# Gated delta-rule kernel: the broadcast of the pair rows in two parts by rows, two transfers under way at most, and beta multiplied in part by part

## The chip, the cores and the metric

The kernel runs on one core of a Trainium2 chip. The metric is the device time of one execution in microseconds (us). The engines are TensorE (PE; its weight loads are PEld), VectorE (DVE), ScalarE (ACT), GpSimd (POOL) and SyncE (SP). SP issues most DMAs. Each engine runs its own list of instructions in order and waits on semaphores.

## What is computed

A layer of 16 heads (head size 32) over 4 sequences of 2048 tokens of width 512: layer norm, a gated delta-rule recurrence, output projection, layer norm, residual; then a feed-forward part in which each token takes one of 16 columns. The part that the change touches is the recurrence, cut here from the reference:

```
q, k, v, gate = projections of the normed x;  beta = sigmoid(x @ Wb.T);  alpha = exp(-exp(A_log) * softplus(...))
def step(S, inp):
    k_t, q_t, v_t, beta_t, a_t = inp
    S = S * a_t[..., None, None]
    kv_mem = einsum('bhd,bhde->bhe', k_t, S)
    delta = (v_t - kv_mem) * beta_t
    S = S + k_t[..., :, None] * delta[..., None, :]
    y_t = einsum('bhd,bhde->bhe', q_t, S)
    return (S, y_t)
```

## The kernel before

The 2048 tokens go in 32 blocks of T = 64 (NT = 32), a block in two chunks c = 0, 1 of 32 tokens, a chunk in two halves j = 0, 1 of 16 tokens (CS = 16). A "half (c, j)" below is such a half. All 16 heads of the 4 sequences are done at once: 128 partitions (4 heads times 32 channels) by G = 16 groups.

Within a half the deltas depend on one another through a triangular matrix A (products of keys, with decays). DVE solves it in `solve_half` (L1090 on): it takes S k off v (L1097), multiplies by beta (L1101), and then for t0 = 0 to 14 makes a product `Ut` of row t0 of A with the delta of token t0 (L1108) and subtracts it from the tokens behind (L1111). Each step is done in two `turns` of 8 groups. The rows of A must lie in all 32 channel partitions of a head. For that SP writes A (`Ak`) to DRAM (`write_rows`, L325) and reads it back with a broadcast (`fetch_pairs`, L334) into `pairs[j]`, in 4 transfers, one for each head h, 32 partitions by 15 rows by 1 KB. `pairs[j]` is one buffer for each j, free again (`pairs_free0`, `pairs_free1`) when the solve of that j is done. POOL then multiplies the rows by beta in place (`pairs_times_beta`, 15 instructions, L940) and signals `pr_ready`.

The program is a software pipeline written out by hand: in `step`, every engine works on one block's recurrence ("chain"), on the next block's projections ("ahead"), on the block behind (outputs, "after") and on the one behind that ("late"). The order of each engine's instructions is fixed there. On SP it is, from the solve of (0, 0) on: fetch (0, 1), load the residual (L341), write rows of chunk 1, fetch (1, 0), fetch (1, 1), load x of the next block (L320), write rows of chunk 0 of the next block, store (L347), fetch (0, 0) of the next block.

Two more things are used below. First, `vb_free`: ACT writes the next block's beta (`sigmoid("beta", ...)`, L789) over the present one's, so it first waits for `vb_free`, which DVE signals in the last solve of a block, (1, 1), with the second multiply by beta (L1101). That multiply first takes `pr_ready`, and so POOL, which also reads beta, is done with it as well. Second, the PSUM banks `work`: three of them, taken in turn (`TURNS`, `BANK`); PE waits in `into` until the use before has been read. The second transposition for the gate network (`turn("xfT", xfw, 1)`, L443) takes the bank that the first sigmoid of beta reads.

PE's list around the end of a block is: `turn xfT 0`, `project beta` (L426), `state_to_outputs` (L481), `turn xfT 1` (L443), `project v` (L426, 8 matmuls), `state_to_outputs` (L481), `project v` (16 matmuls), `change_state(1, 0)` (L493, needs the solved deltas `delT`), `gate_hidden` (L532), `change_state(1, 1)`, `project v` (8), then of the next step `state_to_u(0, 0)` (L466), `gate_logits` (L542, L545), `state_to_u(0, 1)`, `gate_logits`, `turn xT` (L443), `chunk_to_outputs` (L486), `project qk` (L426), `key_products` (L458), `output squares` (L519), `log_alpha` (L500) and `first_half_to_u` (L474), for which DVE's next half waits.

Of the kernel before, what the change touches and what calls it, by code (L numbers as in the profile page):

```python
# [48 lines left out]
PAIRS_IN = 16 * HP  # L49

# [36 lines left out]
def sandwich_kernel(nc, x, w_in, wa, dt_bias, a_log, norm_w, wo, bo, col_emb, gw1, gb1, gw2, gb2,  # L87
                    w_cols, b_cols, proj_w, proj_b, ln_g, ln_b,
                    c_sq, c_sel, c_mask, c_iota, c_pad, c_tok, c_row, c_col, out, xs_dram):
    with ExitStack() as ctx:  # L90
# [128 lines left out]
        def in_qr(*shape, dt=F32):  # L219
# [43 lines left out]
            rows_out0 rows_out1 pairs_free0 pairs_free1 pairs_in0 pairs_in1  # L263
# [49 lines left out]
        def _(sp):  # L313
# [14 lines left out]
            def fetch_pairs(c, j):  # L328
                if not j:
                    take(sp, f"rows_out{c}", 16)  # L330
                take(sp, f"pairs_free{j}", free=1)
                for h in range(HP):
                    rows = pair_rows[c, j, h, j * CS:j * CS + CS - 1, 0:G * CS]
                    sp.dma_start(pairs[j][DH * h:DH * h + DH, 0:CS - 1].rearrange("p s g t -> p s (g t)"),  # L334
                                 rows.unsqueeze(0).to_broadcast([DH, CS - 1, G * CS])).then_inc(s[f"pairs_in{j}"], 16)
# [584 lines left out]
        def _(pool):  # L920
# [13 lines left out]
            def pairs_times_beta(c, j):  # L934

                take(pool, f"pairs_in{j}", PAIRS_IN)
                for t0 in range(CS - 1):
                    a = pairs[j][:, t0, :, t0 + 1:CS]
                    t = c * C + j * CS + t0 + 1
                    ins = nc.gpsimd.tensor_tensor(a, a, beta[:, :, t:t + WID[t0]], ALU.mult)  # L940
                ins.then_inc(s["pr_ready"], 1)
# [110 lines left out]
        def _(dve):  # L1052
# [37 lines left out]
            def solve_half(c, j):  # L1090
# [7 lines left out]
                for i, g in enumerate(turns):  # L1098
                    if i:
                        take(dve, "pr_ready")  # L1100
                    link(v.tensor_tensor(uk[:, g, h], uk[:, g, h], beta[:, g, th], ALU.mult),  # L1101
                         "vb_free" if i and (c, j) == (NC - 1, 1) else None, behind=1, hold=True)

                for t0 in range(CS - 1):
                    n, at = WID[t0], j * CS + t0
                    pr = pairs[j][:, t0, :, t0 + 1:CS]
                    for g in turns:
                        link(v.tensor_tensor(Ut[:, g, 0:n], pr[:, g], uk[:, g, at:at + 1].to_broadcast([P, G // 2, n]),  # L1108
                                             ALU.mult), behind=1)
# [296 lines left out]
```

## Time and profile before

| | us |
|---|---|
| median of 3 runs | 3594.3 (3582.41 to 3595.7) |
| the profiled execution | 3601.23 |
| its span | 3599.1 |
| PE busy | 3056.9 (85%) |
| DVE busy | 2835.6 (79%) |
| POOL busy | 1907.8 (53%) |
| ACT busy | 1312.0 (36%) |

The profiled execution is 6.9 us above the median. PE and DVE are both busy most of the time, and they hand the work to each other several times in a block, so the time is that of a chain that goes through both. The mean granted clock of PE is 0.908 of full speed; the two levels seen in the rows are 1.00 (2.4 GHz) and 0.50 (1.2 GHz). A block takes about 97 us; the recurrence runs from about 95 us to 3140 us of the span, and what follows is the feed-forward part by columns, which the change does not touch.

### The profile page before, as it was taken

How to read it: one execution, taken by the hardware profiler on the slowest of the kernel's cores; microseconds unless marked ns; L12 is line 12 of the kernel's file. 1: busy time of each engine (PE TensorE's matmuls, PEld its weight loads, DVE VectorE, ACT ScalarE, POOL GpSimd, SP SyncE). 2: the span in 40 equal slices, each digit the busy share in tenths (PEclk: the TensorE clock that was granted, in tenths of full speed). 3: DMA queues.
4: the chain of work that ended last, by engine and by line, in shares of the span. 5: the costliest groups of instructions: out<-in, count | busy, mean ns of one | idle time of the engine just before them, and what ended most of it. 6: DMA issues, size and time to landing. Idle time of an engine off the chain costs nothing.

```text
span 3599.1 us, 140793 instructions
## 1 busy us (share of the span) xinstructions
PE 3056.9 (85%) x59368; PEld 2336.8 (65%) x59368; DVE 2835.6 (79%) x12375; ACT 1312.0 (36%) x2520; POOL 1907.8 (53%) x2903
## 2 busy tenths in 40 slices
PE   5889898989988989899989989888899999546774
PEld 4667666667776767677667667666677777434443
DVE  1678787788887888888888788778888888857897
ACT  2233333333333333333333333333333333225664
POOL 1455554555555554555545455555555555415887
PEclk9899899999999999999999999999999999768887
DMA  3655555555555665555565555555565555735774
GB/s 111 120 113 107 97 120 119 111 111 110 113 107 107 120 119 107 108 107 107 110 120 119 108 111 109 112 102 116 119 119 108 109 110 102 151 123 116 129 125 70
DMA packets 341830, 404.78 MB, mean 112 GB/s; under 512 B 22976, under 2 KB 285760, under 8 KB 340688
## 3 DMA queue, kind: packets, MB, share of 16 engines
q1 hardware_dynamic: 324560, 362.07, 49.8%
q0 software_dynamic: 16640, 33.71, 5.1%
q8 instruction: 468, 7.67, 1.0%
q14 instruction: 162, 1.33, 0.1%
HBM read 323.97 MB, written 75.93 MB: 111 GB/s over the span
## 4 chain that ended last, share of the span: by engine, by line
DVE 49%; PE 38%; issue 7%; ACT 3%; POOL 1%; ACTq 1%; DMA 0%; SPq 0%; DVEq 0%; POOLq 0%
PE work L426 11%; DVE uk L1111 10%; DVE Ut L1108 10%; PE work L532 3%; DVE stats L1066 3%; DVE nt L1062 3%; PE work L542 3%; DVE kq L1124 2%; PE uk L466 2%; PE kkq L458 2%; DVE ve L1071 2%; DVE delT L1113 2%; PE work L519 2%; PE work L443 2%; PE uq L486 2%
## 5 line engine op out<-in xcount | busy, mean ns | idle before, releaser
L940 POOL TENSOR_TENSOR pairs<-pairs,beta 128x240 f32<-128x240 f32 (+14 forms) x1920 | 861.6, 489 | 852.3 <-DMA pairs<-pair_rows 852.2
L426 PE MATMUL work<-xT,w_sb 128*128 128x256 f32 x5120 | 1296.2, 402 | 10.0 <-issue 7.6
L426 PEld LDWEIGHTS work<-xT,w_sb 128*128 128x128 f32 x5120 | 978.0, 198 | 183.5 <-issue 39.9
L1111 DVE TENSOR_TENSOR uk<-uk,Ut 128x120 f32<-128x120 f32 (+14 forms) x3840 | 706.4, 225 | 0.0
L1108 DVE TENSOR_TENSOR Ut<-pairs,uk 128x120 f32<-128x120 f32 (+14 forms) x3840 | 686.2, 214 | 1.1
L466 PE MATMUL uk<-kqd,S 32*32 32x32 f32 x8192 | 128.7, 203 | 140.0 <-issue 127.9
L524 PE MATMUL work<-wo_sb,ctxT 128*128 128x512 f32 x512 | 239.9, 612 | 8.5 <-POOL ctxT L959 6.1
L951 POOL TENSOR_TENSOR kd<-kd,dec 128x512 f32<-128x512 f32 x64 | 67.9, 1083 | 335.2 <-DVE kd L1197 335.2
L756 ACT ACTIVATE qraw<-work 128x512 f32<-128x512 f32 x128 | 75.9, 593 | 461.9 <-DVE kq L1124 319.1
L466 PEld LDWEIGHTS uk<-kqd,S 32*32 32x32 f32 x8192 | 103.5, 114 | 181.1 <-issue 178.2
L1118 DVE TENSOR_TENSOR S<-Sd,su 128x512 f32<-128x512 f32 x64 | 44.0, 688 | 180.9 <-PE su L493 180.8
L965 POOL TENSOR_TENSOR xfw<-xfw,pb_sb 128x1024 f32<-128x1024 f32 x32 | 75.4, 2357 | 172.3 <-DVE slot L1182 172.3
L524 PEld LDWEIGHTS work<-wo_sb,ctxT 128*128 128x128 f32 x512 | 93.4, 192 | 107.9 <-issue 97.6
L493 PEld LDWEIGHTS su<-delT,kd 32*32 32x32 f32 x8192 | 83.9, 106 | 111.4 <-issue 59.0
L931 POOL TENSOR_TENSOR kqd<-kq,eg 128x1024 f32<-128x1024 f32 x64 | 150.1, 2346 | 10.0 <-DVE kq L1124 10.0
L1062 DVE SCALAR_TENSOR_TENSOR nt<-nt,ve 128x2 f32<-128x2 f32 x387 | 144.3, 373 | 13.4
L1148 DVE TENSOR_TENSOR lt<-work,gb_sb 128x32 f32<-128x32 f32 x32 | 6.1, 191 | 187.0 <-PE work L545 187.0
L435 PE MATMUL work<-qsq,squares 128*128 128x512 f32 x256 | 150.3, 671 | 0.0
L493 PE MATMUL su<-delT,kd 32*32 32x32 f32 x8192 | 99.4, 195 | 54.4 <-DVE delT L1113 40.1
L763 ACT ACTIVATE qr<-work 128x512 f32<-128x512 f32 x128 | 75.5, 590 | 192.1 <-PE work L435 182.0
L458 PEld LDWEIGHTS kkq<-kq 32*32 32x32 f32 x8192 | 119.4, 105 | 35.3 <-issue 24.8
L750 ACT ACTIVATE xT<-work 128x512 f32<-128x512 f32 x64 | 38.1, 597 | 271.7 <-PE work L443 271.7
(232 smaller groups left out, 5964.3 us busy)
## 6 DMA issues: line engine op xcount, KB each, us to landing
pairs<-pair_rows SPq DMA_DIRECT2D x512, 480.0 KB, 8.3
xt<-in_x SPq DMA_DIRECT2D x66, 256.0 KB
pair_rows<-Ak SPq DMA_DIRECT2D x64, 256.0 KB, 2.3
x<-in_x SPq DMA_DIRECT2D x64, 256.0 KB, 11.9
out<-x SPq DMA_DIRECT2D x64, 256.0 KB, 3.6
wo_sb<-xs_rows SPq DMA_DIRECT2D x30, 258.0 KB
w_sb<-in_w_in SPq DMA_DIRECT2D x1, 5120.0 KB, 14.9
xs_rows<-w_sb SPq DMA_DIRECT2D x17, 258.0 KB, 2.4
```

What stands on the lines that cost most here:

```text
L426: mm = pe.matmul(w[:, half * BT:(half + 1) * BT], w_sb[:, f, j * D + hg * P:j * D + (hg + 1) * P], xT[:, f, :], start=(f == 0), stop=(f == ...
L435: pe.matmul(w, blk1, qsq[n % 2][:], start=True, stop=True).then_inc(s["ss_full"], 1)
L458: on_tiles(half, "kkq_full", lambda g, q, q_half: pe.matmul(kkq[q, g], kq[q, g, c, 0, :], kq[q, g, c].rearrange("p a t -> p (a t)"), start ...
L466: on_tiles(half, "uk_full", lambda g, q, q_half: pe.matmul(uk[q, g], S[q, g, :], kqd[c][q, g, 0, :], start=(g == 0), stop=True, skip_group ...
L493: on_tiles(half, "su_full", lambda g, q, q_half: pe.matmul(su[q, g, :], kd[c][q, g, :], delT[c][q, g, :], start=True, stop=True))
L524: mm = pe.matmul(w, flat(ctxT[:, hg * B + tb * BL:hg * B + (tb + 1) * BL, :]), wo_sb[:, hg, :], start=(hg == 0), stop=(hg == KD - 1))
L532: mm = pe.matmul(w[:, n * BT:(n + 1) * BT], gw1_sb[:, f, n * P:(n + 1) * P], xfT[:, f, :], start=(f == 0), stop=(f == KD - 1))
L931: link(nc.gpsimd.tensor_tensor(kqd[c][:], kq[:, :, c], eg[:, :, c * C:(c + 1) * C].unsqueeze(2).to_broadcast([P, G, 2, C]), ALU.mult), "kq ...
L940: ins = nc.gpsimd.tensor_tensor(a, a, beta[:, :, t:t + WID[t0]], ALU.mult)
L1062: link(v.scalar_tensor_tensor(t, t, -0.5, var, ALU.mult, ALU.mult))
L1108: link(v.tensor_tensor(Ut[:, g, 0:n], pr[:, g], uk[:, g, at:at + 1].to_broadcast([P, G // 2, n]), ALU.mult), behind=1)
L1111: link(v.tensor_tensor(uk[:, g, at + 1:at + 1 + n], uk[:, g, at + 1:at + 1 + n], Ut[:, g, 0:n], ALU.subtract), f"pairs_free{j}" if i and t ...
```

## The change

`fetch_pairs` splits the 15 rows of a half into rows 0 to 6 and rows 7 to 14 (`PARTS`), so there are 8 transfers in place of 4. Before each but the first two, SP waits for the transfer two before it (`OUTSTANDING = 2`). The semaphore `pairs_in{j}` becomes four for each j: one for each part and parity of the head. POOL waits for the first part, multiplies 7 rows, signals `pr_ready`, and does the same with the 8 rows of the second part. DVE takes `pr_ready` before t0 = 0 and before t0 = 7 instead of once before the second multiply by beta; `vb_free` moves from that multiply to the second product `Ut` of t0 = 7, since POOL reads beta until its second part is done. The functions `fetch_pairs`, `pairs_times_beta` and `solve_half` change, nothing else.

```diff
+PARTS = (0, (CS - 1) // 2, CS - 1)
+OUTSTANDING = 2
...
                 take(sp, f"pairs_free{j}", free=1)
-                for h in range(HP):
-                    rows = pair_rows[c, j, h, j * CS:j * CS + CS - 1, 0:G * CS]
-                    sp.dma_start(pairs[j][DH * h:DH * h + DH, 0:CS - 1].rearrange("p s g t -> p s (g t)"),
-                                 rows.unsqueeze(0).to_broadcast([DH, CS - 1, G * CS])).then_inc(s[f"pairs_in{j}"], 16)
+                for n in range(2):
+                    r = slice(PARTS[n], PARTS[n + 1])
+                    for h in range(HP):
+                        ahead = HP * n + h - OUTSTANDING
+                        if ahead >= 0:
+                            take(sp, f"pairs_in{j}{ahead // HP}{ahead % 2}", 16)
+                        rows = pair_rows[c, j, h, j * CS + PARTS[n]:j * CS + PARTS[n + 1], 0:G * CS]
+                        sp.dma_start(pairs[j][DH * h:DH * h + DH, r].rearrange("p s g t -> p s (g t)"),
+                                     rows.unsqueeze(0).to_broadcast([DH, PARTS[n + 1] - PARTS[n], G * CS]))\
+                            .then_inc(s[f"pairs_in{j}{n}{h % 2}"], 16)
...
-                take(pool, f"pairs_in{j}", PAIRS_IN)
-                for t0 in range(CS - 1):
...
+                for n in range(2):
+                    take(pool, f"pairs_in{j}{n}0", PAIRS_IN // 2)
+                    take(pool, f"pairs_in{j}{n}1", PAIRS_IN // 2)
+                    for t0 in range(PARTS[n], PARTS[n + 1]):
...
+                    ins.then_inc(s["pr_ready"], 1)
...
-                for i, g in enumerate(turns):
-                    if i:
+                for g in turns:
+                    link(v.tensor_tensor(uk[:, g, h], uk[:, g, h], beta[:, g, th], ALU.mult), behind=1)
+
+                for t0 in range(CS - 1):
+                    if t0 in PARTS:
                         take(dve, "pr_ready")
-                    link(v.tensor_tensor(uk[:, g, h], uk[:, g, h], beta[:, g, th], ALU.mult),
-                         "vb_free" if i and (c, j) == (NC - 1, 1) else None, behind=1, hold=True)
...
+                    for i, g in enumerate(turns):
+                        link(v.tensor_tensor(Ut[:, g, 0:n], pr[:, g], uk[:, g, at:at + 1].to_broadcast([P, G // 2, n]), ALU.mult),
+                             "vb_free" if i and (c, j, t0) == (NC - 1, 1, PARTS[1]) else None, behind=1, hold=True)
```

How the order on the engines changes, at two places. The first is SP's list from the store of a block to the residual of the next; each row is a DMA, with its shape in partitions, rows and elements, and what SP waits for ahead of it. Before:

```order
L347 DMA out<-x1 64x2x512 [waits x1_ready]
L347 DMA out<-x1 64x2x512
L334 DMA pairs<-pair_rows 32x15x256 [waits pairs_free0,rows_out0]
L334 DMA pairs<-pair_rows 32x15x256 x3
L334 DMA pairs<-pair_rows 32x15x256 [waits pairs_free1]
L334 DMA pairs<-pair_rows 32x15x256 x3
L341 DMA x1<-in_x 64x2x512 [waits store_done,xf_ready]
```

After, for one half:

```order
L341 DMA pairs<-pair_rows 32x7x256 [waits pairs_free0,rows_out0]
L341 DMA pairs<-pair_rows 32x7x256
L341 DMA pairs<-pair_rows 32x7x256 [waits pairs_in000]
L341 DMA pairs<-pair_rows 32x7x256 [waits pairs_in001]
L341 DMA pairs<-pair_rows 32x8x256 [waits pairs_in000]
L341 DMA pairs<-pair_rows 32x8x256 [waits pairs_in001]
L341 DMA pairs<-pair_rows 32x8x256 [waits pairs_in010]
L341 DMA pairs<-pair_rows 32x8x256 [waits pairs_in011]
L341 DMA pairs<-pair_rows 32x7x256 [waits pairs_free1]
```

SP now stays with a half until the sixth of its eight transfers has landed, and only then comes to what stands behind. The second place is DVE's list in the solve of (1, 1), where `vb_free` is signalled: the row that waits for `vb_free` is the one right behind the instruction that signals it. Before:

```order
L1097 TENSOR_TENSOR uk<-vT,uk 128x8x16 [waits corr_full]
L1097 TENSOR_TENSOR uk<-vT,uk 128x8x16 [waits dve_step]
L1101 TENSOR_TENSOR uk<-uk,beta 128x8x16 [waits dve_step]
L1101 TENSOR_TENSOR uk<-uk,beta 128x8x16 [waits pr_ready,dve_step]
L1108 TENSOR_TENSOR Ut<-pairs,uk 128x8x15 [waits vb_free]
L1108 TENSOR_TENSOR Ut<-pairs,uk 128x8x15 [waits dve_step]
```

After (the rows for t0 = 1 to 5 left out where the "..." stands):

```order
L1111 TENSOR_TENSOR uk<-uk,beta 128x8x16 [waits dve_step] x2
L1119 TENSOR_TENSOR Ut<-pairs,uk 128x8x15 [waits pr_ready,dve_step]
L1119 TENSOR_TENSOR Ut<-pairs,uk 128x8x15 [waits dve_step]
L1122 TENSOR_TENSOR uk<-uk,Ut 128x8x15 [waits dve_step] x2
...
L1119 TENSOR_TENSOR Ut<-pairs,uk 128x8x8 [waits pr_ready,dve_step]
L1119 TENSOR_TENSOR Ut<-pairs,uk 128x8x8 [waits dve_step]
L1122 TENSOR_TENSOR uk<-uk,Ut 128x8x8 [waits vb_free]
```

`vb_free` now stands behind seven rounds of products and subtractions and the two products of the eighth. The lists of PE and ACT keep their order and their waits.

## Rows read from the trace of the kernel before

**Rows 1.** The page: chain that ended last; then DMA queues (packets, MB, share).

```profile
DVE 49%; PE 38%; issue 7%; ACT 3%; POOL 1%; ACTq 1%; DMA 0%; SPq 0%; DVEq 0%; POOLq 0%
...
q8 instruction: 468, 7.67, 1.0%
```

**Rows 2.** Who waited for whom: us in total, times, longest us.

```profile
PE uk L466 <- issue: 127.9, 89, 5.5
...
ACT beta L789 <- DVE uk L1101: 83.3, 31, 9.8
...
PE work L443 <- ACT beta L789: 56.6, 28, 2.4
```

**Rows 3.** PE, one block's end: start us, duration, ..., [idle before <-releaser].

```profile
1806.33 0.75 PE L481 MATMUL uq<-kqd,S 32*32 32x32 f32 x64
1809.38 0.66 PE L443 MATMUL work<-squares,xfw 128*128 128x128 f32 x4 [2.30 <-ACT beta L789]
1809.87 1.99 PE L426 MATMUL work<-xT,w_sb 128*128 128x256 f32 x8
...
1817.97 0.75 PE L493 MATMUL su<-delT,kd 32*32 32x32 f32 x64 [1.77 <-DVE delT L1113]
...
1828.82 0.21 PE L466 MATMUL uk<-kqd,S 32*32 32x32 f32 x1 [3.17 <-issue]
1828.95 1.89 PE L542 MATMUL work<-ceT,xfT 128*128 128x16 f32 x8
```

**Rows 4.** DVE, the solve of (1, 1) and what follows.

```profile
1808.21 0.49 DVE L1101 TENSOR_TENSOR uk<-uk,beta 128x128 f32<-128x128 f32 x2
...
1813.35 0.35 DVE L1108 TENSOR_TENSOR Ut<-pairs,uk 128x64 f32<-128x64 f32 x2
...
1823.10 0.69 DVE L1118 TENSOR_TENSOR S<-Sd,su 128x512 f32<-128x512 f32 x1 [5.18 <-PE su L493]
...
1835.93 0.48 DVE L1097 TENSOR_TENSOR uk<-vT,uk 128x128 f32<-128x128 f32 x2
...
1853.93 0.49 DVE L1097 TENSOR_TENSOR uk<-vT,uk 128x128 f32<-128x128 f32 x2 [2.35 <-PE uk L474]
...
1880.03 0.46 DVE L1097 TENSOR_TENSOR uk<-vT,uk 128x128 f32<-128x128 f32 x2
```

**Rows 5.** ACT, the sigmoids of beta.

```profile
1808.73 1.09 ACT L789 ACTIVATE beta<-work 128x512 f32<-128x512 f32 x2 [2.73 <-DVE uk L1101]
```

**Rows 6.** PE, an earlier block's end, the same places as rows 3.

```profile
1616.15 3.20 PE L426 MATMUL work<-xT,w_sb 128*128 128x256 f32 x8
...
1624.24 0.75 PE L493 MATMUL su<-delT,kd 32*32 32x32 f32 x64 [0.26 <-DVE delT L1113]
...
1632.55 0.64 PE L466 MATMUL uk<-kqd,S 32*32 32x32 f32 x52 [1.05 <-issue]
...
1639.68 1.89 PE L542 MATMUL work<-ceT,xfT 128*128 128x16 f32 x8 [3.44 <-issue]
```

**Rows 7.** Stretches: PE, PEld, DVE, ACT, POOL busy (x), PE clock, DMA share, GB/s.

```profile
1826.00:1828.00 2.00, 0.00 (x0) 0.00 (x0) 1.97 (x2) 1.02 (x2) 2.00 (x2) 1.00 1.13 187
...
1836.00:1838.00 2.00, 2.00 (x74) 1.67 (x76) 2.00 (x12) 1.31 (x3) 0.85 (x4) 0.50 0.00 0
```

**Rows 8.** SP's DMAs in the same block.

```profile
1804.95 14.34 SPq L334 DMA_DIRECT2D pairs<-pair_rows  x8
...
1846.50 0.38 SPq L325 DMA_DIRECT2D pair_rows<-Ak  x1
1850.37 15.79 SPq L334 DMA_DIRECT2D pairs<-pair_rows  x8
1875.56 1.25 SPq L320 DMA_DIRECT2D xt<-in_x  x2
```

**Rows 9.** POOL in the same block: rows times beta of (0, 0) and (1, 0).

```profile
1818.84 6.46 POOL L940 TENSOR_TENSOR pairs<-pairs,beta 128x240 f32<-128x240 f32 x15 [17.87 <-DMA pairs<-pair_rows]
...
1862.98 6.86 POOL L940 TENSOR_TENSOR pairs<-pairs,beta 128x240 f32<-128x240 f32 x15 [8.05 <-DMA pairs<-pair_rows]
```

More of the change, by code:

```diff
@@ L262, in sandwich_kernel @@
             oh_ready rank_full rank_read slot_ready scat_done
-            rows_out0 rows_out1 pairs_free0 pairs_free1 pairs_in0 pairs_in1
+            rows_out0 rows_out1 pairs_free0 pairs_free1 pairs_in000 pairs_in001 pairs_in010 pairs_in011 pairs_in100 pairs_in101 pairs_in110 pairs_in111
             ce_sq ce_n ce_T base_ready setup_v setup_a cnt_ready table_ready
@@ L331, in fetch_pairs @@
                 take(sp, f"pairs_free{j}", free=1)
-                for h in range(HP):
-                    rows = pair_rows[c, j, h, j * CS:j * CS + CS - 1, 0:G * CS]
-                    sp.dma_start(pairs[j][DH * h:DH * h + DH, 0:CS - 1].rearrange("p s g t -> p s (g t)"),
-                                 rows.unsqueeze(0).to_broadcast([DH, CS - 1, G * CS])).then_inc(s[f"pairs_in{j}"], 16)
+                for n in range(2):
[8 more added lines that the diff above has]
+                            .then_inc(s[f"pairs_in{j}{n}{h % 2}"], 16)
+                for odd in range(2):
+                    seen[sp, f"pairs_in{j}1{odd}", ""] += 16
             def load_residual(i):
@@ L934, in pairs_times_beta @@
             def pairs_times_beta(c, j):
-                take(pool, f"pairs_in{j}", PAIRS_IN)
-                for t0 in range(CS - 1):
[L938 to L941, printed above, removed]
+                for n in range(2):
+                    take(pool, f"pairs_in{j}{n}0", PAIRS_IN // 2)
+                    take(pool, f"pairs_in{j}{n}1", PAIRS_IN // 2)
+                    for t0 in range(PARTS[n], PARTS[n + 1]):
+                        a = pairs[j][:, t0, :, t0 + 1:CS]
+                        t = c * C + j * CS + t0 + 1
+                        ins = nc.gpsimd.tensor_tensor(a, a, beta[:, :, t:t + WID[t0]], ALU.mult)
+                    ins.then_inc(s["pr_ready"], 1)
             def step(p, chain, after, ahead, late, added):
@@ L1097, in solve_half @@
                     link(v.tensor_tensor(uk[:, g, h], vT[:, g, th], uk[:, g, h], ALU.subtract), behind=1)
-                for i, g in enumerate(turns):
-                    if i:
+                for g in turns:
+                    link(v.tensor_tensor(uk[:, g, h], uk[:, g, h], beta[:, g, th], ALU.mult), behind=1)
+                for t0 in range(CS - 1):
+                    if t0 in PARTS:
                         take(dve, "pr_ready")
-                    link(v.tensor_tensor(uk[:, g, h], uk[:, g, h], beta[:, g, th], ALU.mult),
-                         "vb_free" if i and (c, j) == (NC - 1, 1) else None, behind=1, hold=True)
-                for t0 in range(CS - 1):
                     n, at = WID[t0], j * CS + t0
                     pr = pairs[j][:, t0, :, t0 + 1:CS]
-                    for g in turns:
-                        link(v.tensor_tensor(Ut[:, g, 0:n], pr[:, g], uk[:, g, at:at + 1].to_broadcast([P, G // 2, n]),
-                                             ALU.mult), behind=1)
+                    for i, g in enumerate(turns):
+                        link(v.tensor_tensor(Ut[:, g, 0:n], pr[:, g], uk[:, g, at:at + 1].to_broadcast([P, G // 2, n]), ALU.mult),
+                             "vb_free" if i and (c, j, t0) == (NC - 1, 1, PARTS[1]) else None, behind=1, hold=True)
                     for i, g in enumerate(turns):
```

## The prediction

> **What bounds the kernel now.** Read first the chain that ended last [rows 1]: 49% of the span lies on DVE, 38% on PE, 7% on "issue", hardly anything on POOL, SP or a DMA. So a faster transfer buys nothing by itself, and what counts is how DVE and PE hand over in a block. Read next one block in order of time. DVE solves (1, 1) from 1808 on and then waits 5.18 us for PE's change of state [rows 4]. From 1817.97 PE leads: change of state, gate network, next states [rows 3]. DVE follows it until 1853.93, where it has waited 2.35 us for PE [rows 4]. From there to the next solve of (1, 1) DVE leads. A delay of PE between 1817.97 and 1853.93 therefore goes into the period whole, and so does a gain, as long as DVE's wait lasts.
>
> Three more things are to be seen in PE's rows. PE waits for beta: 2.30 us ahead of the turn at 1809.38 [rows 3], 28 times, 56.6 us in all [rows 2]. It then has 1.77 us left before the deltas are there at 1817.97; in another block only 0.26 us, because its 8 matmuls behind the wait took 3.20 us and not 1.99 [rows 3, 6]. And in `state_to_u` it stands for nothing that the profile names, 3.17 us here, 127.9 us in all at that line [rows 2, 3]. That wait falls into the broadcast: DMA share is 1.13 at 187 GB/s while PE does nothing [rows 7]. Two such waits in a row end 7.1 us apart (1632.55 and 1639.68) [rows 6]. I read them as instructions that come late: PE's next instructions travel on the same DMA engines (the instruction queue of [rows 1]) as the broadcast.
>
> **Part 1: the transfers themselves.** Before, 4 transfers of a half take from 1850.37 until POOL goes on at 1862.98, 12.6 us; for (0, 0) 13.9 us [rows 8, 9]. After, two at a time. The nearest row for "issue, land, issue the next" is the write of 256 KB: issued at 1846.50, next issue at 1850.37, 3.9 us [rows 8]. Four such rounds are 15.5 us; if the two of a round do not overlap fully, I add 1.2 us each (a quarter MB at about 200 GB/s) and get 20 us. So a half lands 3 to 7 us later than now, its first part after 8 to 10 us. Who notices? (0, 0): lands by 1825, first needed at 1835.93. (1, 0): lands by 1870.4, and POOL's second part, about 3 of its 6.86 us, ends by 1873.5, needed at 1880.03 and then only for t0 = 7 on [rows 4, 9]. (0, 1) starts when its buffer is free at 1817 and SP has finished with (0, 0), lands by 1840, needed at 1853.93. (1, 1) likewise has some 20 us. All hidden: cost 0. With rounds beyond 6 us (24 us a half) (1, 0) would begin to touch the solve.
>
> Behind the waits on SP are queued the residual, the write of chunk 1 and the load of x. The load of x is issued at 1875.56 now, when the decays are ready [rows 8]; SP would come to it at 1879 to 1882, and DVE reads x only after 1900. The write of chunk 1 at 1846.50 comes after SP is free (about 1836). Cost 0.
>
> **Part 2: two takes of `pr_ready` on DVE.** Both are long satisfied. The multiply by beta that has the wait now takes as long as its neighbours (the two of them 0.49 us) [rows 4], so a satisfied wait costs nothing that shows; bounds 0 to 0.05 us for each of 128 more, at most 6 us. I take 0. The multiplies on POOL are the same 15.
>
> **Part 3: `vb_free` moves.** This is a cost that the title does not tell. DVE's second multiply by beta ends at 1808.70 (1808.21 + 0.49) and ACT's sigmoid starts at 1808.73 [rows 4, 5]. Now the signal comes with the second product of t0 = 7, which ends at 1813.70 (1813.35 + 0.35) [rows 4]: 5.0 us later. ACT is idle there, so beta comes 5.0 us later, and the turn goes from 1809.38 to 1814.4. Behind it PE has fixed work until the change of state: 8.6 us from the turn to 1817.97 (and from 1615.66 to 1624.24 when the clock is low), of which 1.77 and 0.26 us are waiting [rows 3, 6]. Lower bound: 5.0 - 1.77 = 3.2 us, with the clock untouched. But PE now idles 7.3 us in place of 2.3, and already after 2.3 us the following matmuls ran at half the clock in some blocks (3.20 against 1.99 us) [rows 3, 6]. Then the slack is eaten and the whole 5.0 us pass; if the low level lasts longer, 5.9. I take 5.0, the value to which the 1.2 us of lost clock and the lower bound nearly add up. It occurs in the 31 blocks that have a next block: +155 us (bounds +99 and +183).
>
> **Part 4: instructions come sooner.** Now up to 4 transfers of 0.49 MB are queued; at 190 to 200 GB/s that is 10 us of data in front of whatever comes behind. With two of about 0.25 MB it is at most 2.5 us. The wait at L466 is 127.9 / 32 = 4.0 us a block [rows 2]. A fetch took 7.1 us under the full queue [rows 6]. If 5 of these were queueing, they fall to about 1.3, and the fetch to 3.5 us; PE goes through such a stretch in 3 to 4 us, so about 1 us of waiting stays. Gain 3.0 us a block; bounds 0 (the queue's depth does not matter) and 4.0 (all). After the wait the clock stands at 0.50 for some 10 us [rows 7], and the small matmuls behind take 1.89 us for 8 [rows 3]. Without any wait this could give back up to 3.6 us more a block, from what PE's stretch takes (29.2 us from 1817.97 to `first_half_to_u`) less 3.2 us of wait and 21.8 us for the same groups at the full clock (my sum). But the stretch is thin work, and another low phase is likely there anyway; I take 0.5 us, bounds 0 and 3.6. Sum: -3.5 us in 32 blocks, -112 us (bounds 0 and -243).
>
> A rule speaks against the gain. In the trace the waits lie under the broadcast [rows 3, 7], but no row shows the order within a DMA engine. The Trainium skill (DMA: Bandwidth & Descriptors, Queues, rings and completion order) says that each engine goes round-robin between its queue rows, packet by packet. A fetch of instructions would then wait for little more than one packet of the broadcast, however many transfers are queued, and Part 4 would be 0 but for the thinner load; the 7.1 us of rows 6 speak against that. It is the second rival below.
>
> **Sum.** +155 - 112 = +43 us. On the profiled execution, 3601.2, that is 3644; the median is 6.9 us lower, so **3637**.
>
> **Rivals.**
> 1. The waits for instructions go, and the clock with them (other side, faster). 4.0 + 3.6 = 7.6 us in 32 blocks are 243 us, less 155: 88 us faster, 3506. With half of the clock's share, 3565. It decides from 4.9 us a block on, where both terms are equal. For it: the waits stand only under the full queue. Against it: the thin matmuls, and that the load of the DMA engines now lasts longer, 30 us in place of 25, so more of PE's list lies in it.
> 2. Depth does not matter: only Part 3 is left, 3594.3 + 155 = 3749.
> 3. The later beta is absorbed, since DVE's own path is nearly as long (DVE's waits before the turn to PE are 5.18 and 2.35 us [rows 4]): then only 3.2 us or less pass, and with -3.5 the time stays the same, 3585 to 3600. Against it: the 5.18 us are themselves a wait for PE.
> 4. The halves land late after all, from 24 us on: each further us on (1, 0) costs 32 us, from 3750 up. Against it: margins of 7 us and more.
>
> **How the numbers follow.** Forecast, both terms in their middle (3600 to 3700, 3637 the value): 0.44. Rival 1 (3506 to 3576): 0.28. Rival 2 (3720 to 3777): 0.18. Rival 3: 0.07. Rival 4: 0.03. The range leaves out the outer half of rivals 1 and 2: 3530 to 3752. Faster by over 0.5% (below 3576): 0.29; within 0.5%, about what a measurement of this kernel can tell: 0.13; slower: 0.58. The likeliest case alone is 3600 to 3700.
>
> **What the profile after would show.** Right: ACT waits some 7.7 us for DVE at the sigmoid of beta (now 2.73), PE about 7.3 us at the second turn (now 2.30), in 31 blocks; the wait for `delT` before L493 is gone, and DVE's wait for S grows from 5.2 to about 10 us; waits at L466 for "issue" fall from 127.9 to some 30 us; SP's transfers of a half spread over 15 to 20 us with a DMA share well under 1.1; DVE shows no wait for POOL. Wrong: waits at L466 unchanged (rival 2), PE's clock high through the stretch (rival 1), POOL or DVE waiting for `pairs` after 1880 (rival 4).

## The result, and the profile after

The changed kernel takes **3560.8 us** (median of 5 runs, 3559.69 to 3565.62) against 3589.7 us (median of 5, 3582.41 to 3595.7) for the kernel before: a ratio of 0.992, 95% interval 0.990 to 0.994. It is 0.8% faster. The prediction was 3637 us and "slower" as the likeliest side; the time lies in the range (3530 to 3752), but the side was wrong.

First the page of the changed kernel: span, busy time, queue of the transfers, the chain, and the two groups of broadcasts (KB each, median us from issue to landing).

```profile
span 3558.4 us, 141657 instructions
...
PE 2971.8 (84%) x59368; PEld 2266.6 (64%) x59368; DVE 2901.1 (82%) x12375; ACT 1308.1 (37%) x2520; POOL 1905.3 (54%) x2903
...
DVE 62%; PE 28%; issue 4%; ACT 3%; POOL 1%; ACTq 1%; DMA 1%; DVEq 0%; SPq 0%; POOLq 0%
...
pairs<-pair_rows SPq DMA_DIRECT2D x512, 256.0 KB, 3.4
...
pairs<-pair_rows SPq DMA_DIRECT2D x512, 224.0 KB, 3.7
```

The chain has moved from PE to DVE: 62% and 28% in place of 49% and 38% [rows 1], and "issue" fell from 7% to 4%. PE's busy time is 85 us less with the same matmuls, so they ran at a higher clock (mean granted clock 0.922, before 0.908).

Then who waited for whom (us in total, times, longest us).

```profile
POOL pairs L952 <- ACT beta L799: 428.6, 31, 14.2
DVE S L1129 <- PE su L503: 316.5, 33, 10.3
ACT beta L799 <- DVE Ut L1119: 243.1, 31, 14.7
PE work L453 <- ACT beta L799: 215.1, 30, 7.3
...
PE uk L484 <- DVE delT L1124: 40.0, 24, 7.3
...
PE uk L476 <- issue: 10.7, 15, 1.9
```

Against [rows 2]: ACT now waits 7.8 us a block for DVE (2.7 before), because `vb_free` hangs on the second product `Ut` of t0 = 7. PE waits 7.2 us a block for beta (2.0 before). And PE's waits for "issue" in `state_to_u`, which the prediction read as late instructions, have nearly gone: 10.7 us in 15 times, where there were 127.9 us in 89. POOL's first row shows the later beta as well; it costs nothing there, since POOL is waited for nearly nowhere (DVE waits for it 1.4 us in the whole execution).

The same in one block, PE's rows (start, duration, ..., idle before), to be held against [rows 3]:

```profile
1782.36 1.11 PE L453 MATMUL work<-squares,xfw 128*128 128x128 f32 x4 [7.17 <-ACT beta L799]
1783.27 3.49 PE L436 MATMUL work<-xT,w_sb 128*128 128x256 f32 x8
...
1791.03 0.75 PE L503 MATMUL su<-delT,kd 32*32 32x32 f32 x64
...
1797.97 0.75 PE L476 MATMUL uk<-kqd,S 32*32 32x32 f32 x64
1798.65 1.06 PE L552 MATMUL work<-ceT,xfT 128*128 128x16 f32 x8
...
1805.36 3.69 PE L436 MATMUL work<-xT,w_sb 128*128 128x256 f32 x16 [0.93 <-DVE lt L1161]
...
1815.37 0.72 PE L484 MATMUL uk<-Ak,delT 16*32 16x16 f32 x64 [1.68 <-DVE delT L1124]
```

Two things are to be seen. Behind the wait of 7.17 us the 8 matmuls of `project v` take 3.49 us (1.99 in rows 3); the granted clock is 0.56 from 1783 to 1787 us, and back at 1.00 after that. The change of state follows 8.67 us behind the turn with no wait for `delT`. Then `state_to_u` goes through in one piece, 64 matmuls without the wait of 3.17 us, and the 8 small ones behind it take 1.06 us in place of 1.89.

Two rows of the stretches (columns as in rows 7) show the broadcast under that same stretch: PE is busy throughout at the full clock, with a DMA share of about 0.7 where it was 1.13.

```profile
1797.00:1799.00 2.00, 2.00 (x72) 1.56 (x71) 1.97 (x2) 1.53 (x3) 2.00 (x2) 1.00 0.65 213
...
1801.00:1803.00 2.00, 2.00 (x20) 1.97 (x19) 1.89 (x4) 0.19 (x1) 2.00 (x4) 1.00 0.74 189
```

Last SP's queue and POOL a little later, (1, 0) and (1, 1) in the 16 issues:

```profile
1819.08 24.35 SPq L341 DMA_DIRECT2D pairs<-pair_rows  x16
1843.48 1.25 SPq L322 DMA_DIRECT2D xt<-in_x  x2
```

```profile
1826.82 3.98 POOL L952 TENSOR_TENSOR pairs<-pairs,beta 128x240 f32<-128x240 f32 x7 [2.86 <-DMA pairs<-pair_rows]
...
1834.37 2.73 POOL L952 TENSOR_TENSOR pairs<-pairs,beta 128x128 f32<-128x128 f32 x8 [3.58 <-DMA pairs<-pair_rows]
```

The first part is there 7.7 us after the first issue, the second after 15.3 us (12.6 before, [rows 8, 9]).

**Where the time went, by stages.** The block can be cut at DVE's rows: the four times that the deltas are transposed (`delT`: 00, 01, 10, 11, by half) and the two additions to the state (S, S'). The table has the mean us between these marks over 28 blocks. The stage S' to 00 is the one from the second addition to the first `delT` of the next block. The kernels of the experiments stand in the table too; they are told below. Of e10 the full name is `e10_early_out8_whole_beta`.

| kernel | 00 to 01 | 01 to S | S to 10 | 10 to 11 | 11 to S' | S' to 00 | period |
|---|---|---|---|---|---|---|---|
| before | 17.46 | 10.24 | 16.16 | 24.70 | 6.32 | 21.67 | 96.56 |
| changed | 16.80 | 9.02 | 15.85 | 24.86 | 10.71 | 18.33 | 95.56 |
| e1_early_vb | 17.11 | 9.14 | 15.87 | 24.85 | 6.18 | 17.76 | 90.91 |
| e2_late_vb_only | 17.58 | 10.43 | 16.45 | 24.60 | 11.30 | 19.64 | 100.00 |
| e3_all_eight | 17.46 | 9.09 | 16.06 | 24.78 | 10.83 | 19.31 | 97.53 |
| e4_two_whole | 18.41 | 9.97 | 16.12 | 24.72 | 6.23 | 18.54 | 93.99 |
| e7_early_out8 | 17.40 | 8.98 | 16.00 | 24.82 | 6.21 | 20.49 | 93.89 |
| e8_early_out4 | 17.28 | 8.97 | 15.88 | 24.86 | 6.24 | 18.37 | 91.61 |
| e9_one_row | 16.58 | 8.86 | 15.87 | 24.87 | 6.40 | 18.34 | 90.91 |
| e10 (whole beta) | 18.44 | 9.99 | 15.91 | 24.87 | 6.00 | 19.76 | 94.96 |

In the changed kernel 11 to S' grew by 4.4 us (the late beta). From S' to 01, which is the stretch that PE leads, the block is 4.0 us shorter: 3.3 us in S' to 00 and 0.7 us in 00 to 01, where DVE waits 1.2 us a block less for PE. 01 to S shrank by 1.2 us, and there DVE hardly waits at all, before or after: its own instructions take 1.0 us less (why is told under the multiply by beta). With the small rest of -0.15 that is -1.0 us a block, 31 us in 31 blocks; 29 were measured.

In S' to 00 a second thing is to be seen. DVE waited there for PE, 5.9 us a block (its wait ahead of L1148, the gate's logits). In the changed kernel it waits for nothing, 0.02 us a block, because its own instructions now fill the stage: they take 2.5 us more. The wait in the whole execution (us in total, times, longest us), first the kernel before, then the changed one:

```profile
DVE lt L1148 <- PE work L545: 187.0, 32, 10.7
```

```profile
DVE lt L1159 <- PE work L555: 11.7, 3, 10.7
```

So DVE bounds that stage now, and PE can give no more there.

### The profile page after: what moved, and what is told of

The parts are those of the page before. It is cut to its first block, busy times and chain, and to the rows that moved or that the text cites. A ratio compares the mean times of both kernels' runs of the same rounds, so it can differ in the third digit from the quotient of the medians.

```text
span 3558.4 us, 141657 instructions
## 1 busy us (share of the span) xinstructions
PE 2971.8 (84%) x59368; PEld 2266.6 (64%) x59368; DVE 2901.1 (82%) x12375; ACT 1308.1 (37%) x2520; POOL 1905.3 (54%) x2903
## 3 DMA queue, kind: packets, MB, share of 16 engines
q1 hardware_dynamic: 332752, 362.10, 40.6%
## 4 chain that ended last, share of the span: by engine, by line
DVE 62%; PE 28%; issue 4%; ACT 3%; POOL 1%; ACTq 1%; DMA 1%; DVEq 0%; SPq 0%; POOLq 0%
DVE uk L1122 12%; DVE Ut L1119 12%; PE work L436 12%; DVE nt L1074 4%; DVE nt L1073 4%; DVE stats L1078 4%; PE work L542 3%; DVE kq L1135 3%; DVE ve L1083 2%; DVE delT L1124 2%; DVE uk L1109 1%; PE su L503 1%; PE work L453 1%; ACT kq L899 1%; PE uk L484 1%
## 5 line engine op out<-in xcount | busy, mean ns | idle before, releaser
L436 PE MATMUL work<-xT,w_sb 128*128 128x256 f32 x5120 | 1323.5, 409 | 20.9 <-DVE lt L1161 12.4
L436 PEld LDWEIGHTS work<-xT,w_sb 128*128 128x128 f32 x5120 | 1002.6, 203 | 202.2 <-issue 47.4
L453 PE MATMUL work<-squares,xfw 128*128 128x128 f32 x256 | 57.3, 365 | 237.1 <-ACT beta L799 215.1
L453 PEld LDWEIGHTS work<-squares,xfw 128*128 128x128 f32 x256 | 37.1, 181 | 241.6 <-ACT beta L799 218.4
L1074 DVE SCALAR_TENSOR_TENSOR nt<-nt,ve 128x2 f32<-128x2 f32 x387 | 158.3, 409 | 13.4
L445 PE MATMUL work<-qsq,squares 128*128 128x512 f32 x256 | 141.9, 637 | 20.4 <-ACT qsq L767 20.3
L936 POOL TENSOR_TENSOR Sd<-S,eg_end 128x512 f32<-128x512 f32 x64 | 67.8, 1059 | 161.8 <-DVE S L1129 161.8
L468 PE MATMUL kkq<-kq 32*32 32x64 f32 x8192 | 135.8, 217 | 18.1 <-DVE kq L1135 16.8
L484 PEld LDWEIGHTS uk<-Ak,delT 16*32 16x32 f32 x8192 | 81.9, 106 | 89.7 <-issue 89.3
L799 ACT ACTIVATE beta<-work 128x512 f32<-128x512 f32 x64 | 34.8, 595 | 251.2 <-DVE Ut L1119 243.1
```

The costliest lines, as they stand in the source:

```text
L436: mm = pe.matmul(w[:, half * BT:(half + 1) * BT], w_sb[:, f, j * D + hg * P:j * D + (hg + 1) * P], xT[:, f, :], start=(f == 0), stop=(f == ...
L445: pe.matmul(w, blk1, qsq[n % 2][:], start=True, stop=True).then_inc(s["ss_full"], 1)
L453: mm = pe.transpose(w[:, half * BT + tb * P:half * BT + (tb + 1) * P], src[:, tb, f * P:(f + 1) * P], ident)
L468: on_tiles(half, "kkq_full", lambda g, q, q_half: pe.matmul(kkq[q, g], kq[q, g, c, 0, :], kq[q, g, c].rearrange("p a t -> p (a t)"), start ...
L1074: link(v.scalar_tensor_tensor(t, t, -0.5, var, ALU.mult, ALU.mult))
```

## The experiments

Theory: the late `vb_free` costs about 5 us a block, and fewer transfers in flight let PE's instructions come sooner, with the clock that goes with it. "The throttle" below is SP's wait that lets at most two transfers be under way. Rivals: the depth of the queue does not matter (only the thinner load or nothing does), or the late beta is absorbed. The runs of the kernel before beside each group had medians of 3590.3 to 3593.0 us.

### The late signal alone, with and without the throttle

`e1_early_vb` is the changed kernel with the signal back where it was:

```diff
+                last = (c, j) == (NC - 1, 1)
+                for i, g in enumerate(turns):
+                    if i and last:
+                        take(dve, "pr_ready", 2)
+                    link(v.tensor_tensor(uk[:, g, h], uk[:, g, h], beta[:, g, th], ALU.mult),
+                         "vb_free" if i and last else None, behind=1, hold=True)
...
-                    if t0 in PARTS:
+                    if t0 in PARTS and not last:
                         take(dve, "pr_ready")
```

> The changed kernel, but in the last solve of a block, (1, 1), DVE takes both pr_ready before its second multiply by beta, and signals vb_free there, as the kernel before does. All else as changed: 8 transfers, two under way. Theory A (the late vb_free costs 5.0 us a block less the mean slack of about 1 us; the throttled transfers give the gain): PE waits about 2.3 us for beta instead of 7.2, and the time falls by 31 x 4 = 120 us from 3561 to about 3440. Rival B (the wait for beta shelters PE: when the thin matmuls come 5 us earlier they meet the broadcast of (0, 1) at its start and wait for instructions again): waits at state_to_u come back to 2 us or more a block, time 3490 to 3560. Rival C (DVE is the bound by now, the wait for beta is absorbed): within 10 us of the changed kernel.

Measured: **3405.7 us** (3393.14 to 3417.01), ratio 0.947 (0.945 to 0.949). It is 155 us faster than the changed kernel, and faster than the kernel before too. The expectation of about 3440 was 34 us too high. Who waited for whom:

```profile
DVE S L1133 <- PE su L503: 175.5, 33, 7.7
...
PE work L453 <- ACT beta L799: 55.3, 30, 2.3
...
PE uk L476 <- issue: 38.7, 69, 1.5
```

PE's wait for beta is back at 1.8 us a block, DVE's for PE's change of state falls by 141 us. The table puts 4.5 of the 4.65 us of the period into 11 to S'.

`e2_late_vb_only` is the kernel before with nothing changed but the place of the signal:

```diff
-                         "vb_free" if i and (c, j) == (NC - 1, 1) else None, behind=1, hold=True)
+                         behind=1)
...
                         link(v.tensor_tensor(Ut[:, g, 0:n], pr[:, g], uk[:, g, at:at + 1].to_broadcast([P, G // 2, n]),
-                                             ALU.mult), behind=1)
+                                             ALU.mult),
+                             "vb_free" if i and (c, j, t0) == (NC - 1, 1, 7) else None, behind=1, hold=True)
```

> The kernel before, with only vb_free moved from the second multiply by beta to the second product of t0 = 7 in the solve of (1, 1). Transfers and POOL as before. Theory A: the turn waits 7.2 us for beta, PE comes 3.2 to 5.0 us later to the change of state, and nothing is given back: +4 to +5 us in 31 blocks, 3590 + 124 to 155 = 3714 to 3745. Rival C: absorbed, 3590 to 3610. Rival D (the longer idle time of PE lets it collect instructions, so part of the waits at state_to_u goes with it): those waits fall from 4 us a block to 2 or less, time 3640 to 3690.

Measured: 3686.4 us (3679.28 to 3698.46), ratio 1.025 (1.024 to 1.027): 94 us slower, not 155. Its waits:

```profile
DVE S L1119 <- PE su L493: 331.0, 33, 12.5
ACT beta L789 <- DVE Ut L1108: 227.2, 31, 14.7
PE work L443 <- ACT beta L789: 191.0, 30, 7.2
...
PE uk L466 <- issue: 83.2, 88, 5.7
```

The time falls in the range of rival D (3640 to 3690). The late beta costs 5.0 us in 11 to S', but 2.0 us come back in S' to 00: PE's waits for "issue" at the line fall by 45 us, to 2.6 us a block (rival D had 2 or less). That they fall because PE comes to `state_to_u` when more of the broadcast is through is an argument, not shown by itself. Under the throttle those waits are nearly gone already, and the cost is whole.

`e3_all_eight` is the changed kernel without the throttle (`OUTSTANDING = 2` to `8`), all 8 transfers issued at once.

> The changed kernel with OUTSTANDING = 8: the same 8 transfers in two parts, beta part by part, late vb_free, but SP waits for none of them. Theory A (how much is queued decides): waits at state_to_u are back at about 4 us a block and the time is that of the late vb_free alone, 3714 to 3745. Rival E (the splitting, or POOL's multiply part by part, made the gain): within 20 us of the changed kernel's 3561.

Measured: 3620.8 us (3617.02 to 3628.9), ratio 1.008 (1.007 to 1.010), so the throttle is worth 60 us in the changed kernel. Both forecasts missed: theory A had 3714 to 3745, rival E within 20 us of 3561. Some of the gain is the throttle's and some is there without it, which the later runs take apart. PE's waits at `state_to_u` are there again:

```profile
PE work L453 <- ACT beta L799: 202.3, 30, 7.3
...
PE uk L476 <- issue: 73.2, 89, 5.7
```

### The throttle alone

`e4_two_whole` leaves the 4 transfers and the multiply in one piece, and only issues them two at a time:

```diff
+OUTSTANDING = 2
...
                 for h in range(HP):
+                    if h >= OUTSTANDING:
+                        take(sp, f"pairs_in{j}{h % 2}", 16)
```

> The kernel before with its 4 whole transfers a half, SP letting only two be under way, POOL and vb_free as before (once for a half). Up to 0.98 MB is queued where it was 1.97 and is 0.5 in the changed kernel. Theory A (bytes in the queue): a fetch of instructions waits up to 5 us; waits at state_to_u fall to 1.5 to 2.5 us a block, time about 3590 - 32 x 3.5 = 3480 (3450 to 3530). Rival F (the number of transfers, not their bytes): as good as the changed kernel with early vb_free, about 3440. If depth does not matter: 3590.

Measured: 3503.4 us (3492.29 to 3511.81), ratio 0.975 (0.973 to 0.976). The wait at the line is 59.5 us:

```profile
PE uk L471 <- issue: 59.5, 94, 4.7
```

So a throttle without any split gives 89 us: S' to 00 is 3.1 us a block shorter, and 1.0 us is lost again in 00 to 01, where DVE waits for PE.

### How many under way, with the early signal

Three kernels with the early signal of `e1_early_vb` and `OUTSTANDING` at 8, 4 (with a semaphore for each transfer) and 1.

> The early vb_free of e1 with OUTSTANDING = 8: 8 transfers in two parts, none of them waited for by SP, beta part by part. With e1, the changed kernel and e3 it makes a square of throttle by vb_free. Theory A (what is queued ahead of an instruction fetch decides; eight issues of about 0.85 us pace the queue, four whole ones do not): the gain of e3 over e2 (66 us) is that of the pacing, so this is 3592 - 66 = 3526 (3510 to 3540). Rival G (the splitting gives nothing by itself, e3's 66 us come from the shifted beta): 3580 to 3595. Rival H (the throttle adds nothing once it is split): 3406 as e1.

> As e1, but four of the eight transfers under way, each with its own semaphore: about 0.98 MB queued at most, as much as in e4 with its two whole transfers, in twice the number. Theory A (bytes in the queue): like e4, 3503, or up to 25 us under it for the finer grain: 3475 to 3510. Rival F (number of transfers under way): as the unthrottled kernel before, which also has four under way, near e7, 3525 to 3590. If one more round of depth costs nothing: 3406.

> As e1, but OUTSTANDING = 1: each of the eight transfers lands before the next is issued. A transfer alone takes about 3.4 us from issue to the next issue, 27 us a half, 110 us for the four halves of a block, more than e1's period of 91 us. Theory K (SP's chain of round trips becomes the bound, DVE and POOL wait for pairs): period 112 to 120 us, time 4050 to 4350. Rival L (the round trips are short enough to hide, and the queue is emptier still): within 20 us of e1.

| under way | us (median, lowest to highest) | ratio (95%) | `state_to_u` waits for issue: us, times, longest |
|---|---|---|---|
| 8 | 3508.9 (3503.44 to 3515.76) | 0.978 (0.976 to 0.979) | 95.0, 75, 5.2 |
| 4 | 3426.1 (3412.46 to 3433.69) | 0.953 (0.950 to 0.955) | 51.2, 81, 2.8 |
| 2 | 3405.7 (3393.14 to 3417.01) | 0.947 (0.945 to 0.949) | 38.7, 69, 1.5 |
| 1 | 3994.2 (3987.85 to 3995.75) | 1.113 (1.110 to 1.115) | 4.1, 6, 1.5 |

The rows of the waits are, for 8 and for 4:

```profile
PE uk L476 <- issue: 95.0, 75, 5.2
```

```profile
PE uk L476 <- issue: 51.2, 81, 2.8
```

The same bytes in the same number of packets (332752 on the queue of the transfers, 362.10 MB) go in every row of the table. How many of them are queued differs, and the longest wait goes down with it, 5.2, 2.8, 1.5 us.

A throttle also spreads the broadcast, so its rate could be what counts, and not how much is queued. For 8 against 4 the traces settle that: the transfers of the halves (0, 0) and (1, 0) are through after 12.4 and 12.2 us with 8 under way and after 12.7 and 12.2 us with 4 (medians from the first issue to the last landing), which is the same rate, and yet the time falls by 83 us, and PE's stretch from the change of state to `first_half_to_u` from 27.4 to 24.5 us a block. For 4 against 2, 20 us, the rate falls too (16.0 and 15.2 us), and the two are not told apart.

For 8 the expectation was 3526 (3510 to 3540), and 3508.9 was measured. For 4 it missed: it was to lie near `e4_two_whole` (3503), which has as many bytes queued (two of 0.49 MB), and it is 77 us faster. So the bytes queued are not the whole of it: the longest wait is 4.7 us with two of 0.49 MB and 2.8 us with four of 0.24 MB. The kernels also differ in how beta is multiplied, which is worth 32 us (below); the other 45 us were not taken apart.

With one under way the waits at the line are gone as well, but SP's round trips are the bound: the period is 108.2 us (112 to 120 expected, and 4050 to 4350 us for the time, so the side was right and the size too large). The first row is SP's issue of two halves, the two others who waited for whom:

```profile
1852.28 45.91 SPq L341 DMA_DIRECT2D pairs<-pair_rows  x16
```

```profile
POOL pairs L952 <- DMA pairs<-pair_rows: 1814.7, 225, 19.6
...
PE work L534 <- POOL ctxT L971: 391.7, 32, 17.4
```

Each transfer is issued 2.9 us after the one before (45.91 / 16). Four halves are 92 us, and with x and the writes SP alone needs more than the 91 us that a block takes in `e1_early_vb`. DVE then waits for POOL's rows, 207.9 us in all.

`e9_one_row` asks what is left to gain. After the first fetch into each buffer, a transfer brings only the first row of its part; it leaves out the other rows, so its output is not the reference's.

```diff
+                    stop = PARTS[n + 1] if full else PARTS[n] + 1
+                    r = slice(PARTS[n], stop)
```

> As e1, but after the first fetch into each of the two buffers a transfer brings only the first row of its part, so 2 rows of 15 come instead of all; the other rows of pairs stay as they are, are multiplied and used by the same instructions, and the output is not the reference's. It shows what is left when the broadcast no longer loads the DMA engines. Theory A: the waits of PE for nothing named at state_to_u go to nearly 0 (38.7 us in e1), the stretch from change_state to first_half_to_u falls from 24.7 us to 22 to 23.5, and the time from 3406 to 3340 to 3380. Rival I (these waits are not a matter of DMA load, but of PE's own stream, and the throttle helped otherwise): waits and time as in e1, within 15 us.

Measured: 3411.6 us (3406.1 to 3416.24), ratio 0.950 (0.948 to 0.952), the same as `e1_early_vb` within what the runs tell, and its wait is nearly the same too:

```profile
PE uk L479 <- issue: 34.9, 70, 1.5
```

With two under way the volume of the broadcast costs no time any more. The expectation (3340 to 3380, and a PE stretch of 22 to 23.5 us) missed: the stretch is 23.7 us, 23.9 in `e1_early_vb`, and the rival stands, that the short waits that remain are not the volume's. The time alone would not show it, since in `e9_one_row` DVE waits for nothing in S' to 00 and so hides what PE may have gained.

### The multiply by beta in parts

`e10_early_out8_whole_beta` is `e7_early_out8` with POOL multiplying all 15 rows in one go behind the second part, and one `pr_ready`:

```diff
-                    for t0 in range(PARTS[n], PARTS[n + 1]):
...
+                for t0 in range(CS - 1):
```

> As e7 (eight transfers, no throttle, early vb_free), but POOL waits for all eight, multiplies the 15 rows in one go and signals pr_ready once, and DVE takes it once before the second multiply by beta, as in the kernel before. It takes the part-by-part beta out of e7. Theory A: the part-by-part beta gives nothing, since DVE does not wait for pairs: within 10 us of e7. Rival J (POOL's rows times beta lie elsewhere in time and disturb DVE's copies and norms less when they are done in parts): 20 us or more above e7.

Measured: 3541.1 us (3535.29 to 3546.23), ratio 0.985 (0.983 to 0.987). The beta in parts is therefore worth 32 us (theory A, within 10 us, fell), and splitting the transfers without any throttle or change to the multiply is worth 52 us against the kernel before.

By stages the period falls by 1.07 us: 1.01 us in 01 to S; in S' to 01, taken as one, only 0.3 us (0.7 more in S' to 00, 1.0 less in 00 to 01, where DVE came later and so waited less for PE). What changed in these stages is in DVE's groups (us in total, mean ns). `lt` are small operations on the gate's logits, `kq` the scaled keys and queries, `nt` a step in the inverse root of a variance, the same code in both kernels. First `e10`, then `e7`:

```profile
L1137 DVE TENSOR_TENSOR kq<-qraw,qr 128x512 f32<-128x512 f32 x128 | 107.6, 859 | 19.6 <-ACT qr L774 19.6
...
L1073 DVE TENSOR_TENSOR nt<-c_rstd 128x2 f32<-128x2 f32 x96 | 51.8, 539 | 3.3
...
L1172 DVE TENSOR_SCALAR lt<-lt 128x32 f32<-128x32 f32 x32 | 11.8, 368 | 1.1
...
L1166 DVE TENSOR_SCALAR lt<-lt 128x32 f32<-128x32 f32 x32 | 11.1, 345 | 0.2 <-ACT lt L814 0.2
```

```profile
L1139 DVE TENSOR_TENSOR kq<-qraw,qr 128x512 f32<-128x512 f32 x128 | 102.9, 822 | 16.7 <-ACT qr L774 16.7
...
L1073 DVE TENSOR_TENSOR nt<-c_rstd 128x2 f32<-128x2 f32 x96 | 99.8, 1040 | 3.3
...
L1168 DVE TENSOR_SCALAR lt<-lt 128x32 f32<-128x32 f32 x32 | 6.3, 196 | 0.2 <-ACT lt L814 0.2
...
L1174 DVE TENSOR_SCALAR lt<-lt 128x32 f32<-128x32 f32 x32 | 6.1, 192 | 1.1
```

The same 32 instructions `lt` take 0.36 us each in one kernel and 0.19 us in the other. Six such groups of `lt` sum to 63.2 and 41.5 us, `kq` to 107.6 and 102.9: 26 us, and all of it lies on DVE's own path in 01 to S. `nt`, in S' to 00, goes the other way: 51.8 and 99.8 us. There DVE waited for PE anyway, 4.1 us a block in `e10`, so only the 0.7 us arrives. In both cases what differs is what POOL does beside them. In the kernel before, POOL multiplies (1, 0) from 1862.98 to 1869.84 [rows 9], and DVE's operations start under it. First the kernel before, then the changed one, where POOL has paused between its parts (both rows of the same instruction):

```profile
1863.83 0.52 DVE L1153 TENSOR_SCALAR lt<-lt 128x32 f32<-128x32 f32 x1
```

```profile
1832.06 0.14 DVE L1164 TENSOR_SCALAR lt<-lt 128x32 f32<-128x32 f32 x1
```

This one takes 0.38 us longer while POOL works, less than one of POOL's multiplies of those rows (3.98 / 7 = 0.57 us).

In S' to 00 the same is to be seen larger, in `nt`, DVE's instruction of two elements a partition. First the kernel before, where POOL is still multiplying the rows of (0, 0) until 1825.30 [rows 9]; then two rows of the changed kernel, where POOL is through with those rows and starts `Sd` and `kqd` together with DVE:

```profile
1824.39 0.23 DVE L1061 TENSOR_TENSOR nt<-c_rstd 128x2 f32<-128x2 f32 x1
```

```profile
1798.04 2.27 DVE L1073 TENSOR_TENSOR nt<-c_rstd 128x2 f32<-128x2 f32 x1
```

```profile
1797.94 2.35 POOL L941 TENSOR_TENSOR kqd<-kq,eg 128x1024 f32<-128x1024 f32 x1
```

DVE's instruction ends 0.02 us after POOL's (1800.31 and 1800.29), and the one before it did so too (`c_rstd`, 1.05 us beside POOL's `Sd` of 1.06). With no POOL instruction beside it `nt` takes 0.16 us. The whole root (`c_rstd` and `nt`) takes 4.7 us a block in S' to 00 in the kernel before, and 7.4 us in the changed one, in `e2_late_vb_only`, `e3_all_eight` and `e7_early_out8`: in these POOL is idle when S' comes (in `e7_early_out8` in all of the 32 blocks but one), be it for the late signal or for the multiply in parts, while it is still at the rows in 26 blocks of the kernel before and in 30 of `e10`.

The Trainium skill (SBUF — State Buffer, SBUF: two separate sides) says that DVE and GpSimd share a pair of ports, which DVE uses with two inputs in SBUF or in a mode that takes both, and that one instruction holds the pair whole, so that the other engine's instruction waits until it has ended. By that rule, the trace agrees: a small operation of DVE is longer by part of one multiply of POOL (0.14 against 0.52 us, 0.16 against 2.27 us), and not by a share of its own length.

### The changed kernel and the best one again, side by side

> The changed kernel once more, on the chip of e1_again and e6, so that the price of the late vb_free under the throttle is read on one chip: 3555 to 3567, ratio to before 0.992.

> e1 once more: changed kernel with the early vb_free. If the price of the late one is 5.0 us in 31 blocks, it lies 155 us under changed_again: 3400 to 3411. If e1's 3406 was helped by its chip: above 3420.

Measured on another chip: the changed kernel 3562.1 us (3556.03 to 3563.15), ratio 0.992 (0.990 to 0.994); the early signal 3413.8 us (3404.9 to 3427.75), ratio 0.952 (0.950 to 0.954), a little above the 3400 to 3411 expected. The late signal costs 148 us here, 155 us by the medians of the first comparison. The waits at the line are, in the changed kernel, 10.6 us in 14 times, as before. In the early signal's they are not as before, though the kernel is the same:

```profile
PE uk L476 <- issue: 11.1, 13, 1.6
```

In the first trace it was 38.7 us in 69 times (that execution took 3417.0 us, this one 3405.3 us). So a difference of some 30 us in the sum of these waits may be chance, as between 4 and 2 under way in the table above; the longest wait, 1.5 and 1.6 us, holds.

### What the runs add up to

From the kernel before to the changed one, by medians:

| step | us | from |
|---|---|---|
| 8 transfers for 4, all at once | -52 | before 3593.0, e10 3541.1 |
| beta multiplied in parts | -32 | e10, e7 3508.9 |
| two under way | -103 | e7, e1 3405.7 |
| `vb_free` late | +155 | e1, changed 3560.8 |

The last two steps cross groups of runs (e1 ran on another chip than e7). By the ratios to the kernel before, two under way is worth 110 us with the first run of e1 (0.978 - 0.947) and 93 us with the second (0.978 - 0.952). The first two steps were measured with the early signal and without the throttle alone. The steps are not independent: the late signal costs 94 us in the old queue, 112 us with 8 at once (e3 and e7), 148 to 155 us with two under way.

## Why the prediction was wrong, point by point

**Part 1, transfers hidden: right.** A half lands after 15.3 us (15.5 to 20 forecast), its first part after 7.7 us (8 to 10). DVE waits for POOL 1.4 us in all. Rival 4 did not occur.

**Part 2, cost 0: this step failed.** The sum had only the two takes, which cost nothing indeed, and "the multiplies on POOL are the same 15". They are, but I did not ask what lies beside them on DVE. Pausing between the parts frees DVE's small operations in 01 to S: from before to changed, the six groups of `lt` fall from 63.9 to 40.4 us and `kq` from 108.0 to 102.1 us, 29 us of DVE's own path, and the stage is 1.2 us a block shorter. The runs put the term at -32 us. That alone carries the forecast from 3637 to 3605, the side still open. DVE as a whole is not relieved: its busy time rose from 2835.6 to 2901.1 us, mostly since `nt` and its like meet POOL's instructions in S' to 00, which I did not see either.

**Part 3, +155: right.** The runs give 148 and 155. In the stage it is 4.4 to 4.5 us a block and not 5.0; the lower bound of 3.2 us and the 1.2 us of clock add up to just that. ACT waits 7.8 us (7.7 forecast), PE 7.2 (7.3), DVE's wait for S is 9.6 us (10). The size was right only because the throttle works: in the old queue the same step costs 94. Rival 3 (absorbed) fell.

**Part 4, -112: right in the waits, wrong in the size of the clock's term.** In PE's stretch from the change of state to `first_half_to_u`, 29.3 us before and 24.6 after, the waits for "issue" fall from 3.9 to 0.8 us a block, by 3.1 where 3.0 was forecast. What PE takes without any wait falls from 25.3 to 22.35 us, by 2.9, where I had put 0.5: the stretch stands at 1.00 where it stood at 0.50. (The bound of 3.6 for this term was a wrong sum: 29.2 less 3.2 and 21.8 is 4.2.) And 1.3 us come back as waits for DVE, seen in the 0.93 and 1.68 us of the rows above. Of the 4.7 us on PE 4.0 arrive at DVE, in S' to 01. The fall of the waits is not the queue's alone, since the late signal by itself took 45 us off them in the old queue. By the runs the two steps on the queue are 155 us (52 and 103) against 112, if the step to 8 transfers is counted here.

**The sum.** In stages, forecast +1.5 us a block, measured -1.0. Of the 2.5 us between them 1.2 are Part 2's, 0.6 the late beta, 0.5 Part 4's and the rest small. In runs, -32 for Part 2 and 43 more for Part 4 are the 75 us between the sum +43 and the -32 that the steps add up to. The two accounts share the miss out differently, since the steps are not independent; in both, Part 2's term is missing and Part 4's is too small, and neither alone turns the side.

**Rival 2, depth does not matter: fell.** 8 and 2 under way move the same packets and differ by 103 us, and the longest wait goes from 5.2 to 1.5 us; 8 and 4 do so at the same rate and differ by 83 us. The Trainium skill's rule (DMA: Bandwidth & Descriptors, Queues, rings and completion order), from which I had drawn that a fetch waits for little more than one packet, does not hold in that consequence, if the waits are fetches. What the order within a DMA engine is no run shows.

**Rival 1** (3506 to 3576) had the right side and held the time, by a partly other way and so partly by luck: the waits and the clock gave PE 6.0 of the 7.6 us, 1.3 of them came back as waits for DVE, and Part 2 gave some of what was lacking.

**What stays open.** That the waits are fetches of instructions is inferred: no row names them; they shrink with the depth of the queue, and when PE comes to the line later. Why 8 transfers at once are better than 4 of twice the size by 52 us was not tested apart. S' to 00 is 1.9 us shorter and 00 to 01 1.0 us longer; PE's stretch is only 0.8 us shorter, and a half lands no sooner or later (12.2 to 13.1 us against 12.4 to 13.3). SP's issues of a half lie over 3.8 us in place of 1.8, which may pace the queue; that is an argument and not shown. Nor is it known what makes four of 0.24 MB better than two of 0.49 MB.

## What to carry to other kernels

Ask of a bulk transfer not only when it lands but what it keeps others from: where PE stands for "issue" under a broadcast, issue it in small transfers, two at a time, and stop before the issuing engine's round trips fill the period. When a consumer is split, look at each signal that hung on the whole and keep it where it was if its buffer has another reader behind it; here that one line took back 155 of 187 us. And when work moves on POOL, look in every stage at DVE's small operations beside it: here they lost 1.0 us a block in one stage and gained 2.5 us in another, and only the first lay where DVE was the bound before.

## What the hardware showed that I had not expected

- PE's waits for "issue" at one line fall with the number of transfers of about 0.24 MB under way: the longest is 5.2, 2.8, 1.5 us with 8, 4, 2, though 8 and 4 land at the same rate. Bytes alone do not set it: two of 0.49 MB give 4.7 us, four of 0.24 MB 2.8 us. With two under way a broadcast of 2 rows in place of 15 was no faster (3411.6 against 3405.7 us).
- Small DVE operations beside POOL's instructions last until POOL's instruction ends: 0.36 against 0.19 us on the mean beside the multiplies, and 2.27 against 0.16 us for one of 128x2 elements beside a POOL instruction of 2.35 us.
- Transfers of about 0.24 MB follow one another every 2.9 us when each is issued only after the one before has landed, against every 1.5 us with two under way (45.91 and 24.35 us for 16).
